# Routing a two-layer mixture of experts: counting and rounding of slots moved from VectorE integer steps to TensorE sums and fp32 rounding

## The reference

```python
x = x + xattn0(layernorm(x), ctx)         # 16 heads, 77 context rows, rmsnorm on q and k
x = x + moe0(layernorm(x))                # 8 experts, top 2 of softmax(x @ router_w), hidden 256
x = x + linear1(layernorm(x), ctx_mean)   # W1 x + W2 mean(ctx) + b
x = x + moe1(layernorm(x))                # 8 experts, top 2, hidden 1024

# inside a moe, for every token:
logits = x @ router_w
probs = softmax(logits)
top_p, top_e = top_k(probs, 2)
y = sum over the two chosen experts of  top_p * (gelu(x @ w_in[e] + b_in[e]) @ w_out[e] + b_out[e])
```

## Time and profile before

| | |
|---|---|
| median of 3 runs | 676.58 us (676.15 to 679.18) |
| profiled execution: its span | 675.4 us |
| PE busy | 539.1 us (80% of the span) |
| DVE busy | 533.7 us (79%) |
| POOL busy | 380.6 us (56%) |
| ACT busy | 362.7 us (54%) |
| chain that ended last | PE 45%, DVE 25%, POOL 10%, issue 8%, ACT 5%, DMA 4% |

### The profile page before, as it was taken

The page is one execution under the profiler, slowest core; times in us unless marked ns, Lnnn a source line. Parts: engine busy times, 40 slices in busy tenths (PEclk is TensorE's granted clock), DMA queues, the critical chain, the costliest instruction groups (busy, mean ns, idle before and its releaser), DMA issues.

```text
span 675.4 us, 17795 instructions
## 1 busy us (share of the span) xinstructions
PE 539.1 (80%) x6442; PEld 481.7 (71%) x6442; DVE 533.7 (79%) x1111; ACT 362.7 (54%) x574; POOL 380.6 (56%) x317
## 2 busy tenths in 40 slices
PE   6799998989998644789961655269999999999991
PEld 5688898889897532677751444149999999999981
DVE  3669899999898668699985898658888777888861
ACT  1555475756564442699862677305445444445431
POOL 8047698898879421788407884041554446454331
PEclk9899999999798775899995799569999999999997
DMA  8400223232222243799744542542454544445422
GB/s 299 142 17 18 71 56 83 83 92 76 79 87 68 90 115 124 213 292 288 222 157 132 164 115 64 149 82 54 73 81 79 78 74 72 79 79 77 62 25 23
DMA packets 75317, 71.55 MB, mean 106 GB/s; under 512 B 45346, under 2 KB 65571, under 8 KB 74979
## 3 DMA queue, kind: packets, MB, share of 16 engines
q1 hardware_dynamic: 64338, 50.85, 25.9%
q0 software_dynamic: 10896, 19.58, 15.4%
HBM read 44.83 MB, written 16.53 MB: 91 GB/s over the span
## 4 chain that ended last, share of the span: by engine, by line
PE 45%; DVE 25%; POOL 10%; issue 8%; ACT 5%; DMA 4%; DVEq 1%; SPq 1%; POOLq 0%; ACTq 0%
PE banks L1407 43%; POOL rv L579 3%; POOL heads L586 2%; DVE w_region L1030 2%; POOL w_region L593 2%; POOL w_region L598 2%; DVE w_region L1035 2%; DVE heads L1022 2%; ACT slot_region L832 1%; PE banks L1616 1%; DVE w_region L1012 1%; DVE heads L1005 1%; DVE st L911 1%; DVE x_res L1352 1%; POOL wb_region L657 1%
## 5 line engine op out<-in xcount | busy, mean ns | idle before, releaser
L1407 PE MATMUL banks<-w_region 128*128 128x128 f16 (+6 forms) x1964 | 168.3, 245 | 30.9 <-DVE w_region L1035 9.1
L1407 PEld LDWEIGHTS banks<-w_region 128*128 128x128 f16 (+3 forms) x1964 | 153.2, 120 | 44.3 <-DVE w_region L1035 12.4
L1407 PE MATMUL banks<-w_region,wb_region 128*128 (+1 forms) x1000 | 119.4, 277 | 9.9 <-DMA wb_region<-wk 6.8
L670 POOL DMA_INDIRECT out<-slot_region,lg x39 | 63.7, 1633 | 108.1 <-ACT slot_region L879 97.7
L1407 PE MATMUL banks<-slot_region,staging 128*128 128x128 f16 x1872 | 112.2, 220 | 3.7 <-DMA slot_region<-slot_region 3.5
L1407 PEld LDWEIGHTS banks<-w_region,wb_region 128*128 128x128 f16 (+1 forms) x1000 | 100.2, 106 | 20.7 <-issue 10.9
L1407 PEld LDWEIGHTS banks<-slot_region,staging 128*128 128x128 f16 x1872 | 109.0, 99 | 5.7 <-DMA slot_region<-slot_region 4.3
L839 ACT ACTIVATE wb_region<-wb_region 128x1024 f32<-128x1024 f32 x39 | 41.3, 1058 | 126.5 <-DVE wb_region L1249 126.5
L1240 DVE COPY staging<-w_region 128x2048 f16 x78 | 58.3, 749 | 44.3 <-PE banks L1407 43.1
L626 POOL DMA_INDIRECT slot_region<-normed_rows,index x39 | 50.4, 1293 | 34.6 <-DVE index L1215 20.5
L626 POOL DMA_INDIRECT slot_region<-gated_rows,index x39 | 40.1, 1028 | 32.2 <-DVE index L1215 20.6
(11 more groups left out here) (246 smaller groups left out, 996.3 us busy)
## 6 DMA issues: line engine op xcount, KB each, us to landing
staging<-w_t SPq DMA_DIRECT2D x24, 512.0 KB, 4.7
sorted_y<-slot_region SPq DMA_DIRECT2D x39, 128.0 KB, 4.1
w_region<-w_t SPq DMA_DIRECT2D x8, 512.0 KB
x_res<-x SPq DMA_DIRECT2D x4, 512.0 KB, 10.2
staging<-w_in SPq DMA_DIRECT2D x4, 512.0 KB, 4.3
normed_rows<-w_region SPq DMA_DIRECT2D x16, 128.0 KB, 1.9
staging<-w_out SPq DMA_DIRECT2D x4, 512.0 KB, 3.8
gated_rows<-wb_region SPq DMA_DIRECT2D x16, 128.0 KB, 2.3
```

The source lines that it names most:

```text
L670: g.indirect_dma_start(out=out, out_offset=bass.IndirectOffsetOnAxis(ap=back[:, j:j + 1], axis=0), in_=m.y[:, j % m.YB, 0, :], in_offset=N ...
L1407: return t.matmul(o, a, b, start=start, stop=stop)
```

## The change

Four things are edited, in both routings.

1. **Counts on PE.** `ones`, `before` and `hot` are fp16 in place of fp32. PE no longer gives counts and ranks apart. It makes one table `RANKS` of 17 groups of 8 in PSUM: group t holds, for each expert, the rank inside tile t plus the counts of all lower tiles, and group 16 the totals. It does so by adding `ones` x `hot[i]` onto all groups above i, for each of the 16 tiles, with `hot[i]` read again and again through a broadcast. A matmul of the constant `rounding` comes first and adds 63.5 to the totals.
2. **Rounding in fp32.** Adding and subtracting 1.5 x 2^30 rounds an fp32 number to a multiple of 128. One instruction makes the padded counts, one prefix sum the bases (kept 63.5 lower), and one sum the positions. Two more give `qq` (now 128 times the slot's number, compared with a new constant `iota_s`) and `rr`. The integer form `slots` is written after the one-hots, in the first routing alone.
3. **The choice as its own columns.** `tokens` is positive for both choices. In the second routing the matmuls of the second choice write 78 columns: the token's number in all of them, and once more in columns 39 to 77 as a mark of the second choice. The two instructions that took the sign off are gone.
4. **Small ones.** `masked` is taken from the shifted logits, so that `m2` is already the difference that ACT needs, and L1135 goes. POOL's constants at the start grow by three memsets and an iota.

```diff
+    TO_SLOTS = 1.5 * (P << 23)
+    ALMOST_HALF = P / 2 - 0.5
-        before = sb("before", [P, P], F32)
-        ones = sb("ones", [P, P], F32)
+        before = sb("before", [P, P], F16)
+        ones = sb("ones", [P, P], F16)
+        ones8 = sb("ones8", [P, E], F32)
+        rounding = sb("rounding", [P, NT + 1, E], F16)
+        iota_s = sb("iota_s", [P, max(NQS), 2], F16)
+        RANKS = bank[7][:, 128:128 + (NT + 1) * E].rearrange("p (t e) -> p t e", e=E)
...
             link(g.memset(ones[:, :], 1.0))
+            g.memset(ones8[:, :], 1.0)
+            link(g.memset(rounding[:, :, :], 0.0))
+            g.memset(rounding[0:1, NT, :], ALMOST_HALF)
+            g.iota(iota_s[:, :, :], pattern=[[P, max(NQS)], [0, 2]], base=0, channel_multiplier=0,
+                   allow_small_or_imprecise_dtypes=True)
...
-                link(v.scalar_tensor_tensor(out=te(masked), in0=te(oh[0]), scalar=NEG, in1=cur, op0=ALU.mult, op1=ALU.add))
-                link(v.tensor_reduce(m2, te(masked), axis=AX.X, op=ALU.max))
+                link(v.scalar_tensor_tensor(out=masked, in0=oh[0], scalar=NEG, in1=ex, op0=ALU.mult, op1=ALU.add))
+                v.tensor_reduce(m2, te(masked), axis=AX.X, op=ALU.max).then_inc(sem("route_shift"), 1)
+                dve.wait_ge(sem("route_shift"), 2 * layer + 2)
                 link(v.tensor_tensor(te(cand), te(masked), all_experts(m2), ALU.is_equal))
-                v.tensor_tensor(m2, m2, m1, ALU.subtract).then_inc(sem("route_shift"), 1)
...
                 dve.wait_ge(sem("counts_done"), layer + 1)
-                link(v.tensor_copy(et(tot), bank[7][:, 128:128 + NT * E].rearrange("p (t e) -> p e t", e=E)))
-                link(v.tensor_tensor_scan(incl, ones[:, 0:NT * E], tot, 0.0, ALU.mult, ALU.add))
-                link(v.memset(start[:, 0:1], 0.0))
-                link(v.tensor_copy(start[:, 1:E], ends[:, 0:E - 1]))
-                link(v.tensor_tensor(cnt, ends, start, ALU.subtract))
-                link(v.tensor_scalar(ci, cnt, float(SW - 1), None, ALU.add))
-                link(v.tensor_scalar(ci, ci, SW.bit_length() - 1, None, ALU.logical_shift_right))
-                link(v.tensor_copy(tiles, ci))
-                link(v.tensor_tensor_scan(tend, ones[:, 0:E], tiles, 0.0, ALU.mult, ALU.add))
-                link(v.tensor_tensor(base, tend, tiles, ALU.subtract))
-                link(v.scalar_tensor_tensor(out=base, in0=base, scalar=float(SW), in1=start, op0=ALU.mult,
-                                            op1=ALU.subtract))
-                link(v.tensor_tensor(masked, incl, tot, ALU.subtract))
-                link(v.tensor_tensor(et(masked), et(masked), base[:, :, None].to_broadcast([P, E, NT]), ALU.add))
+                link(v.tensor_scalar(padded, RANKS[:, NT, :], TO_SLOTS, -TO_SLOTS, ALU.add, ALU.add))
+                link(v.tensor_tensor_scan(ends[:, 1:E + 1], ones8[:, :], padded, -ALMOST_HALF, ALU.mult, ALU.add))
-                link(v.tensor_tensor(te(pos), bank[7][:, 256:256 + NT * E].rearrange("p (t e) -> p t e", e=E),
-                                     masked.rearrange("p (e t) -> p t e", e=E), ALU.add))
+                link(v.tensor_tensor(te(pos), RANKS[:, 0:NT, :], base[:, None, :].to_broadcast([P, NT, E]), ALU.add))
...
-                link(v.tensor_copy(slots[:, :, :], hot[:, 0:2 * NT].rearrange("p (c t) -> p t c", c=2)))
-                link(v.tensor_scalar(tiles_of, slots[:, :, :], P.bit_length() - 1, None, ALU.logical_shift_right))
-                link(v.tensor_copy(qq, tiles_of))
-                link(v.tensor_scalar(places, slots[:, :, :], P - 1, None, ALU.bitwise_and))
-                link(v.tensor_copy(rr, places))
+                link(v.tensor_scalar(qq, where, TO_SLOTS, -TO_SLOTS, ALU.add, ALU.add))
+                link(v.scalar_tensor_tensor(out=rr, in0=where, scalar=ALMOST_HALF, in1=qq, op0=ALU.add, op1=ALU.subtract))
...
+                if layer == 0:
+                    link(v.tensor_scalar(slots[:, :, :], where, ALMOST_HALF, None, ALU.add))
...
-                link(v.tensor_scalar(sign, bank[6][:, 0:NQ], 0.0, -2.0, ALU.is_lt, ALU.mult))
-                link(v.scalar_tensor_tensor(out=which, in0=sign, scalar=1.0, in1=bank[6][:, 0:NQ], op0=ALU.add,
-                                            op1=ALU.mult))
-                v.tensor_scalar(index[:, 0:NQ], which, -1.0, 0.0, ALU.add, ALU.max).then_inc(sem("routed"), 1)
+                found, later = bank[6][:, 0:NQ], bank[6][:, NQ:2 * NQ]
+                v.tensor_scalar(index[:, 0:NQ], found, -1.0, 0.0, ALU.add, ALU.max).then_inc(sem("routed"), 1)
...
-                mm(bank[7][:, 128:128 + NT * E], ones[:, :], hot, True, True)
-                mm(bank[7][:, 256:256 + NT * E], before[:, :], hot, True, True).then_inc(sem("counts_done"), 1)
+                mm(RANKS, ones[:, :], rounding[:, :, :], True, False)
+                pe.wait_ge(sem("hot"), layer + 1)
+                mm(RANKS[:, 0:NT, :], before[:, :], hot, False, False)
+                for i in range(NT):
+                    last = mm(RANKS[:, i + 1:NT + 1, :], ones[:, :], hot[:, i:i + 1, :].to_broadcast([P, NT - i, E]),
+                              False, i == NT - 1)
+                last.then_inc(sem("counts_done"), 1)
...
-                    for c in range(2):
-                        last = mm(bank[6][:, 0:NQ], onehots[layer][:, i, :, c], at_q[:, i, :, c],
-                                  i + c == 0, i + c == NT)
+                    for c in (1, 0):
+                        if layer == 1 and c == 1:
+                            last = mm(bank[6][:, 0:2 * NQ].rearrange("p (a q) -> p a q", a=2), onehots[layer][:, i, :, c],
+                                      at_q[:, i:i + 1, :, c].to_broadcast([P, 2, NQ]), i == 0, False)
+                        else:
+                            last = mm(bank[6][:, 0:NQ], onehots[layer][:, i, :, c], at_q[:, i, :, c],
+                                      i == 0 and c == 1, i == NT - 1 and c == 0)
```

More of the change, by code:

```diff
@@ L304, in build, with hot_of @@
         routes = [route0, route1]
+        def hot_of(layer):
+            return routes[layer][:, 640:640 + NT * E // 2].bitcast(F16).rearrange("p (t e) -> p t e", e=E)
         onehots = [onehot0, onehot1]
@@ L1101, in route @@
                 r = routes[layer]
[L1102 removed]
+                NQ, NSLOT = NQS[layer], NSLOTS[layer]
                 def cut(n):
@@ L1138, in route @@
                 link(v.tensor_tensor(te(oh[1]), f8, all_experts(best), ALU.is_equal))
-                v.tensor_tensor(hot, oh[0], oh[1], ALU.add).then_inc(sem("hot"), 1)
+                v.tensor_tensor(hot.rearrange("p t e -> p (t e)"), oh[0], oh[1], ALU.add).then_inc(sem("hot"), 1)
+                padded, ends = counts[:, 0:E], counts[:, 16:16 + E + 1]
+                base = ends[:, 0:E]
                 sums = counts[:, 48:64]
+                v.memset(ends[:, 0:1], -ALMOST_HALF)
                 dve.wait_ge(sem("route_exp"), 2 * layer + 2)
@@ L1180, in route @@
-                link(v.tensor_copy(slots[:, :, :], hot[:, 0:2 * NT].rearrange("p (c t) -> p t c", c=2)))
+                where = r[:, 768:768 + 2 * NT].rearrange("p (c t) -> p c t", c=2)
+                link(v.tensor_reduce(where, both.rearrange("p c (t e) -> p c t e", e=E), axis=AX.X, op=ALU.add))
+                where = where.rearrange("p c t -> p t c")
                 rr, qq = (r[:, k:k + NT].bitcast(F16).rearrange("p (t c) -> p t c", c=2) for k in (1280, 1296))
-                places, tiles_of = (w[:, 0:2 * NT].bitcast(U32).rearrange("p (t c) -> p t c", c=2) for w in (hot, tot))
```

44 lines of the change are left out of this document (20 added, 24 removed).

## The result

| | before | after |
|---|---|---|
| median of 13 runs each, same chip | 676.58 us (673.52 to 683.05) | 671.8 us (667.27 to 674.83) |
| profiled execution: its span | 675.4 us | 669.6 us |

The ratio is 0.9918 with a 95% interval of 0.9897 to 0.9939: faster by 0.8%, more than the 0.5% that a measurement tells from no change. The forecast was 668.9 us in a range of 666.6 to 672.0. The median lies 0.2 us inside the range. Of the forecast gain of 7.7 us only some 5.5 came by the ratio, and 4.8 by the medians.

A forecast was written before the change was run, and what follows sets the result against it. No single engine bounds the whole; in each routing DVE's chain of short dependent instructions holds up everything behind it. Savings of 3.74 us in the first routing and 3.95 in the second, together 7.7, gave 668.9 us, range 666.6 to 672.0.

The forecast's parts named there:

- a: Start of the routing chain: L1135 goes, making the chain 0.09 us shorter.
- c: From the counts to the positions: two of 13 DVE instructions stay, saving 2.77 us in each routing.
- b: Counts on PE: 17 fp16 matmuls take 1.2 us against 1.26 for two fp32 products, taken as no change.
- d: Splitting the position: two of five DVE instructions stay, saving 0.65 us in each routing.
- e: Chain's end: L1212 and L1213 go, saving 0.23 us in first routing, 0.44 in second, where spare time covers 78 columns.
- f: POOL's constants at the start: iota_s 0.5 us and memsets some 0.5 more, hidden; 1.0 us without that cover.
- The copy of the gates: Second routing: the gates' copy to DRAM, 4.4 us to landing, stays hidden by 3 us ahead of `index`.
- each expert stage as long as before: Sign for the stages behind the routings: unchanged length expected.
- rival 1: First expert stage swallows the first routing's gain if weight transfers set its pace: 672.6 us; chance 0.10.
- rival 2: Start of last stage: PE's idle time falls to 2.9 us and the clock may stay up: 667.5 us; chance 0.13.
- the prediction's own last sign: First routing instruction to `index`: a chain not 3.7 to 4.0 us shorter makes the prediction wrong.
- Rival 3: Burst of counts does not pipeline, or the broadcast reads slowly: up to 687.7 us; chance 0.03.

The follow-up runs named there:

- padded: The changed kernel with 18 filler instructions of 8 elements in DVE's chain of each routing; 676.63 us, ratio 1.000 to the kernel before.
- counts_only: The changed kernel with the splitting of the position and the sign of the second choice as before, counts on PE kept; 671.73 us, ratio 0.9915.
- burst_twice: The changed kernel with the constant's matmul and the 17 count matmuls issued twice in each routing; one run, 671.83 us.
- shift15: The changed kernel with 15 one-element memsets that do nothing in DVE's idle waits of the first routing; 670.83 us, ratio 0.9901.
- shift7: The changed kernel with 7 one-element memsets that do nothing in DVE's idle waits of the first routing; one run, 669.4 us.
- idle22_again: The changed kernel with 22 in place of 10 idle matmuls behind the second routing's one-hots, second series; 668.43 us, ratio 0.9883.
- idle22_shift15: The changed kernel with 22 idle matmuls behind the second routing and 15 memsets in the first; 670.66 us, ratio 0.9886.
- after again: The changed kernel once more, unchanged, for a second profile; 669.73 us, ratio 0.990 to the kernel before.
- before, again: The kernel before once more, unchanged, for a second profile; 675.88 us, ratio 0.9987.

## Why the prediction was right, and where it was short

*What bounds the routings.* Right. The chain of short DVE instructions is the time, and all behind it moves with it: padded gives the whole gain back.

*a and c, the counts.* Right: 0.41 us from L1171 to L1174 where 0.42 was said, and 2.94 us for both steps by counts_only. That is 0.08 over 2.86, and most of it is one instruction: the sum that reads PSUM (L1174) takes 0.29 us now and took 0.36 with its transposed table, which I had not counted.

*b, the burst.* Right by its number and by its working: 1.25 us against 1.2, no change. The sum with a floor of 44 ns a narrow matmul held for an operand read through a broadcast. The estimate from the Trainium skill ("TensorE: Matmul & The Clock Gate", section "Back-to-back issue gap"), 1.4 us, was a little high; the second burst of burst_twice has a period of 1.15 us for 18 matmuls, 64 ns each.

*d and e.* Right: 0.44 us for two splits; `index` starts 1.52 us after the last one-hots in the first routing and 1.30 in the second, where 1.5 and 1.3 were said, and DVE is late there, not PE (its matmuls end at 260.83, L1211 starts at 261.58). The forecast that the 78 columns are covered held.

*f, POOL's constants.* Right: iota_s takes 0.56 us, and iota_r starts 0.86 us later than in the earlier trace rows:

```profile
12.90 0.56 POOL L562 IOTA iota_s<- 128x78 f16 x1
...
14.45 1.53 POOL L573 IOTA iota_r<- 128x256 f16 x1
```

ACT's first normalization starts at 22.18 to 24.78 us in the eleven profiles with the new constants (23.83 in after), and at 22.64 to 23.18 in the three without. It can start as early with them as without, so the cover holds.

*The copy of the gates.* Hidden, as said: it took 4.0 us to landing, and POOL was released by `index`.

*What failed: "each expert stage as long as before".* This stood in the working as a cost of zero, and it was 1.0 us in the first and 1.4 us in the last. Both sizes are of two profiles a kernel. Over all profiles with the same instructions in the stage the first holds (a mean of 88.1 in five against 87.0 in three), and the last shrinks: shift15 and shift7 have after's last stage and took 231.56 and 231.23 us, which brings its mean to 231.95, 0.8 over before.
- The first: 1.2 us at three slots, where DVE's sequencer pauses while it loads a register and works with it. It is not rival 1. The rival had transfers for it; over the same 86.81 us from `index` on they moved as much in before (first line) as in after (second line), and 7 memsets took the steps away. That the steps come from the pauses is shown; what the pause is, no run shows.

```profile
266.83:353.64 86.81, 73.57 (x870) 57.65 (x868) 77.90 (x179) 69.85 (x136) 50.41 (x39) 0.96 0.75 229
261.78:348.59 86.81, 73.97 (x870) 57.80 (x868) 76.72 (x177) 68.91 (x136) 47.73 (x39) 0.96 0.74 228
```

- The last: rival 2 had the right place and the wrong sign. It took the idle time ahead of the stage as shorter by the 0.59 us of e and the wider matmuls. It became 0.8 us longer, for two reasons. The idle matmuls were taken to be of a fixed length, and the ten of them took 3.71 us in place of 4.32, since the clock rose 2.9 us after their start (at 439.3) in place of 4.0 (at 447.5); so they end 3.07 us after `index`, and 2.98 before. And PE waits not for `index` but for the first slot's rows and the DMA that transposes them. From `index` to PE's first slot matmul it is 6.50 and 6.58 us in before, and 7.40 and 7.89 in after. The first slot's rows were there at the same distance, and the transpose was issued 3.2 to 3.5 us after `index` in all four. What grew is the time until it landed, in the chain that ended last (start, duration), before and then after:

```profile
448.10 3.14 DMA slot_region<-slot_region
...
440.27 4.12 DMA slot_region<-slot_region
```

In the other profile of each kernel it was 3.07 and 4.68 us. The first matmul came 1.1 us later on the average, and that is most of the 1.4 us. The stretch from it to the end gives the other 0.3, with means of 224.6 us in before and 224.9 in after. But this landing took 3.5 and 3.8 us in shift15 and shift7, 3.0 in burst_twice, and 4.1 and 4.6 in idle22_again and idle22_shift15. The second slot's rows were late too in most kernels with the change and 10 idle matmuls (5.3 to 5.9 us behind `index` in after, after again, shift15, shift7, padded and counts_only, and 4.3 to 4.6 in all others), but the two don't go together: in idle22_again and idle22_shift15 the rows came at 4.5 and 4.4, and the transpose landed as late as in after. What delays either is open: no run isolates the queue. The clock was at half for twice as long in after as in before. That too differs between executions of one kernel (six to seven us in both profiles of after and one of before, again; some three in before, padded, counts_only, shift15, shift7 and idle22_shift15).

7.85 of the routings less 1.0 and 1.4 is 5.4 us, and the medians give 4.8, the ratio 5.5. The term that was missing is one of what follows the shortened chain, not of the chain. By the prediction's own last sign, a chain shorter by 3.7 to 4.0 us, the first routing fits (3.81) and the second is just over (4.04 where 3.95 was summed): each of the two came 0.07 to 0.09 us above its sum.

*Rival 3* is refuted (burst_twice). The outcome that had 0.91, faster, is the one that came. The forecast's own range, 667.4 to 670.4, was too narrow for the medians: two series of after gave 671.8 and 669.7. The wide range held by 0.2 us, a tenth of what two series of one kernel differ by, so that it held is partly luck; its upper end was there for rival 1, which did not happen.

## What to carry to other kernels

Where one engine walks a chain of small dependent instructions, price each by its start-to-start distance in the trace (here 0.21 us for 8 elements, 0.22 for 32 and 0.32 for 128; a prefix sum over 128 took 0.49, and a sum with a transposed table 0.40), and the sum comes out to a tenth of a microsecond. Let an otherwise idle PE form such sums in PSUM: here its 17 matmuls took no longer than the two fp32 products that they replaced, though a second burst would have cost 1.17 us. Then leave some microseconds for the stages behind: removing instructions shifted where DVE's stream pauses, and at the next hand-over a transfer's landing and the clock came out otherwise. Cut such a stage at its first step and compare step by step; that finds what the totals can't.

## What the runs showed of the hardware

- DVE's sequencer pauses for 0.39 us at positions that go by its count of instructions. In the traces it is visible at register loads at the 573rd (padded), 574th (shift7), 700th, 829th and 957th record (after), 126 to 129 apart. The three in after cost 0.40 us each; that at the 957th record of before, also behind a load, cost nothing that its steps show. No run shows what the pause is.
- 17 fp16 matmuls of 8 to 128 columns, each with new weights, take 1.25 us at clock 0.50 from the first to DVE's reading; 16 of them read their moving operand through a broadcast, and the estimate from plain operands was 1.17.
- Whether the clock falls after an idle time of 2 to 4 us is not fixed by its length: 2.08 us with a fall, 3.78 us without. A fall at the start of the last stage cost 1.1 to 2.5 us.
- The DMA that transposes the first slot's rows took 2.9 to 4.7 us from issue to landing in the thirteen profiles in which PE waited for it, issued 3.0 to 3.5 us after `index` in all.
- An fp32 sum of 128x128 with one operand in PSUM takes 0.29 us, and took 0.36 where the other operand was read transposed.
